# A six-layer fused kernel: the recurrence's k plus u is dropped, and the hand order of five engines is replaced

## The reference

```
x = x + attention_0(ln(x))        # 16 heads, weights rounded to -1, 0, 1
x = x + wkv(ln(x), ctx)           # a recurrence over the 128 tokens, per channel
x = x + ffn_0(ln(x))              # 704 hidden, weights rounded to -1, 0, 1
x = x + attention_1(ln(x))        # 32 query heads, 8 key heads
x = x + cross_attention(ln(x), ctx)
x = x + mixture(ln(x))            # low-rank experts, top 2 of 6
```

```
no = max(o, u + k);  A = exp(o - no);  E = exp(u + k - no)
y  = (A p + E v) / (A q + E)
no2 = max(w + o, k); A2 = exp(w + o - no2); E2 = exp(k - no2)
p, q, o = A2 p + E2 v, A2 q + E2, no2
```

## Time and profile before

| | |
|---|---|
| time, median of 3 runs | 685.28 us (684.7 to 687.41) |
| span of the profiled execution | 691.1 us |
| TensorE busy | 613.2 us (89%) |
| VectorE busy | 543.6 us (79%) |
| ScalarE busy | 481.4 us (70%) |
| GpSimd busy | 392.3 us (57%) |
| mean granted TensorE clock | 0.949 |

### The profile page before, as it was taken

One profiled execution on the slowest core, in us unless ns is written; L12 is line 12 of the kernel. 1 busy time (PEld: TensorE's weight loads), 2 busy tenths in 40 slices (PEclk: granted clock), 3 DMA queues, 4 the chain that ended last, 5 costly groups with the idle time before them and its releaser, 6 DMA issues.

```text
span 691.1 us, 20216 instructions
## 1 busy us (share of the span) xinstructions
PE 613.2 (89%) x7368; PEld 372.6 (54%) x7368; DVE 543.6 (79%) x1357; ACT 481.4 (70%) x1185; POOL 392.3 (57%) x745
## 2 busy tenths in 40 slices
PE   6699999856788789999999988789999999999984
PEld 6466666534566568544444344345555556555542
DVE  5889999899899996889998867567777777777521
ACT  4599998996878646577787773467676667666650
POOL 5343786897899958856665312334545544545321
PEclk9799999998899989999999999899999999999995
DMA  8899645111110002444545524353343444433000
GB/s 296 205 220 170 93 94 107 57 58 39 39 39 32 24 11 54 64 78 89 79 79 86 95 58 81 60 89 68 76 82 73 68 80 88 79 76 59 20 9 15
DMA packets 163603, 55.11 MB, mean 80 GB/s; under 512 B 148976, under 2 KB 161456, under 8 KB 163376
## 3 DMA queue, kind: packets, MB, share of 16 engines
q1 hardware_dynamic: 161456, 53.68, 38.1%
q0 software_dynamic: 2048, 0.14, 0.2%
HBM read 16.82 MB, written 5.24 MB: 32 GB/s over the span
## 4 chain that ended last, share of the span: by engine, by line
PE 57%; DVE 18%; issue 7%; POOL 6%; DMA 6%; ACT 4%; SPq 1%; DVEq 0%; ACTq 0%; POOLq 0%
PE bank L1333 4%; PE bank L1266 4%; PE bank L1002 3%; PE bank L1280 3%; PE bank L1678 3%; DMA l1x_qT<-l1x_neg_maxT 3%; DVE mix_num_den L1542 2%; PE bank L1355 2%; PE bank L1305 2%; DMA l1a_kT<-k_stack 2%; PE bank L1287 2%; PE bank L1863 2%; PE bank L976 2%; PE bank L1689 2%; PE bank L1022 2%
## 5 line engine op out<-in xcount | busy, mean ns | idle before, releaser
L1181 DVE TENSOR_REDUCE l1x_neg_max<-bank 128x2 f16<-128x448 f32 (+1 forms) x192 | 116.0, 640 | 46.3 <-PE bank L1287 46.1
L1235 ACT ACTIVATE l1x_probs<-bank 128x512 f32<-128x512 f32 x192 | 104.2, 596 | 57.4 <-PE bank L1309 33.0
L889 DVE TENSOR_REDUCE l1a_neg_max<-bank 128x4 f16<-128x512 f32 x128 | 82.2, 685 | 12.9 <-PE bank L976 11.9
L936 ACT ACTIVATE l1a_probs<-bank 128x512 f32<-128x512 f32 x128 | 69.5, 595 | 21.3 <-PE bank L990 21.3
L1137 POOL DMA_DIRECT2D l1x_qT<-l1x_neg_maxT x64 | 37.5, 592 | 51.7 <-ACT l1x_neg_maxT L1231 51.7
L1678 PE MATMUL bank<-mix_xT_parts,w_ternary 128*128 128x256 f16 x384 | 53.1, 287 | 7.7 <-DVE mix_hidden L1560 7.5
L1678 PEld LDWEIGHTS bank<-mix_xT_parts,w_ternary 128*128 128x128 f16 x384 | 38.5, 103 | 19.8 <-DVE mix_hidden L1560 11.2
L1754 POOL TENSOR_TENSOR moe_logits<-moe_low_rank_logits,router_bias 128x6 f32<-128x6 f32 x16 | 3.3, 206 | 77.4 <-ACT moe_low_rank_logits L1831 77.4
L573 DVE TENSOR_REDUCE l_neg_max<-bank 128x4 f16<-128x512 f32 x64 | 41.5, 674 | 5.7 <-PE bank L698 5.0
L1492 POOL TENSOR_TENSOR mix_hidden_parts<-mix_hidden,mix_hidden_parts 128x256 f16<-128x256 f32 x48 | 38.0, 799 | 8.5 <-ACT mix_hidden_parts L1623 8.1
L642 ACT ACTIVATE l_probs<-bank 128x512 f32<-128x512 f32 x64 | 35.2, 608 | 3.5 <-PE bank L721 1.8
(11 more groups left out here) (271 smaller groups left out, 1814.5 us busy)
## 6 DMA issues: line engine op xcount, KB each, us to landing
ctx_projected<-mix_ctx_projected SPq DMA_DIRECT2D x16, 192.0 KB, 2.0
l1x_ctx_projected<-ctx_projected SPq DMA_DIRECT2D x16, 160.0 KB, 2.4
mix_ctx_in<-ctx_in SPq DMA_DIRECT2D x16, 128.0 KB, 2.1
out_dram<-moe_out SPq DMA_DIRECT2D x16, 128.0 KB, 2.1
x_residual<-x_in SPq DMA_DIRECT2D x1, 1536.0 KB, 10.0
w_f<-w_in SPq DMA_DIRECT2D x2, 704.0 KB, 10.3
w_attn_f<-w_l_in SPq DMA_DIRECT2D x4, 256.0 KB, 3.9
q_stack<-q_begin_in SPq DMA_DIRECT2D x1, 1024.0 KB, 6.2
```

The lines of the kernel that those rows point to most:

```text
L889: dve.tensor_reduce(mm[:, 16 * j + 4 * s:16 * j + 4 * s + 4], b_s[c % 3][:].rearrange("p (r k) -> p r k", k=P), AX.X, ALU.max, negate=True ...
L936: act.activation(prob[:, c, :], b_st[c % 2][:], ACT.Exp).then_inc(s_exp, 1)
L1181: dve.tensor_reduce(mm[:, first:first + count], scores, AX.X, ALU.max, negate=True).then_inc(s_max, 1)
L1235: act.activation(prob[:, c, :], b_st[c % 2][:], ACT.Exp).then_inc(s_exp, 1)
```

## The change

It has three parts.

- k + u is no longer written. `W5` on GpSimd subtracts the running maximum from k itself. u moves into the guard: a tile `limit_minus_u` (60 - u, one column for each channel half, made once by GpSimd) is the bias of the Relu, which therefore runs once for each half.
- Three `F1c` pieces on GpSimd (the layer norm's power) get a further wait, for the normalised x of the sequence before last.
- `PHASES`, `PACE` and `STEPS` have new numbers for `mix`, `l1a`, `l1x` and `moe`, on all engines. `l0` keeps its own.

```
-    ku = sb("k_plus_u", [P, 2, 2, P])
+    spare = sb("limit_minus_u", [P, 2])
...
+        pool.tensor_tensor(spare[:], net.limit[:].to_broadcast([P, 2]), u, ALU.subtract).then_inc(s_c, 1)
...
-                pool.tensor_tensor(dif[:, c, 2], ku[:, c], prev, ALU.subtract).then_inc(s_da, 1)
+                pool.tensor_tensor(dif[:, c, 2], kx[:, c, :, 1:P + 1], prev, ALU.subtract).then_inc(s_da, 1)
...
-                for h in range(2):
-                    act.activation(ku[:, c, h, :], b_kv[c][:, P * h:P * h + P], ACT.Identity, bias=u[:, h:h + 1])
                 act.copy(kx[:, c, :, 1:P + 1], b_kv[c][:, 0:C].rearrange("p (h t) -> p h t", h=2))
...
-                act.activation(room[:, c], flat(dif[:, c, 2]), ACT.Relu, bias=net.limit[:],
-                               scale=-1.0).then_inc(s_ex, 1)
+                for h in range(2):
+                    ins = act.activation(room[:, c, P * h:P * h + P], dif[:, c, 2, h, :], ACT.Relu, bias=spare[:, h:h + 1],
+                                         scale=-1.0)
+                ins.then_inc(s_ex, 1)
...
+                wait(pool, s_xn, b - 1)
                 pool.tensor_tensor(rstd[:, bp, :], ve[:, bp, :], net.mhalf[:], ALU.pow).then_inc(s_rstd, 1)
...
     ("l1a", "pe"): phases("""
-        F5@-0.748 F7@-0.099 S.0@2.190 S.1@2.305 S.2@2.479 S.3@2.759 M@2.913 ST.0@3.547 ST.1@3.789 ST.2@4.136
```

More of the change, by code:

```diff
@@ L160 @@
     ("moe", "pe"): phases("""
[L161 removed]
+        TR@5.208 DOWN@5.245 LORA@5.711 UP@5.969"""),
 }
 PACE = {
[L164 to L168 removed]
+    "l0": (-91.729, 19.870, (4.716, 6.971, 8.492, 11.987), 11.788),
@@ L169 @@
+    "mix": (52.943, 9.367, (10.387, 13.342, 18.920, 10.211), 9.329),
+    "l1a": (155.583, 5.427, (8.962, 8.684, 11.231, 13.171), 11.184),
+    "l1x": (339.807, 9.660, (17.098, 4.845, 5.910, 27.874), 26.177),
+    "moe": (340.648, 2.496, (16.874, 4.857, 5.918, 27.835), 25.791),
 }
```

113 lines of the change are left out of this document (55 added, 58 removed).

## The result

The changed kernel takes 688.72 us in the median of 20 runs (686.58 to 692.53), the kernel before 686.58 us in 20 runs (683.48 to 689.94). The ratio is 1.0031, with a 95% interval of 1.0016 to 1.0046: 2.1 us slower, where I had forecast 3.6 us faster. The difference is smaller than the 0.5% that I called the bound of no change, but it is a difference, and of the other sign. The time lies in the range that I gave; its direction was wrong.

What follows compares the result with a forecast made beforehand. The limit was taken to change between ScalarE, VectorE, GpSimd and TensorE, with TensorE full from about 480 us. Terms -1.2 + 0.1 + 0 - 1.0 - 0.5 - 1.0 = -3.6 took 685.3 to 681.7 us; range 675.5 to 690.5.

Steps and rivals of the forecast that it cites:

- no change: Rival: VectorE and GpSimd take back the 1.2 us saved at the start of `mix`; 684.8 us, chance 0.25.
- Dropped k + u and the Relu halves: Start of `mix`: five Identities leave the chain (-1.61 us), two Relus in halves add 0.44; -1.2 us.
- GpSimd's subtraction: In `mix`, subtracting from k in rows of 129 takes 0.03 us longer, three such steps on the chain; +0.1 us.
- The new order in mix: In `mix`, new neighbours on VectorE and GpSimd neither better nor worse; 0 us, bounds -3.3 and +3.3.
- l1a: -1.0: In `l1a`, a later normalised x waits less for GpSimd's `F8b`; 0.1 us gained in each of ten turns.
- the filled wait: In `l1a`, statistics fill VectorE's wait for TensorE's last `S` before the last two reductions; -0.25 us a turn.
- Change to l1x: At the change to `l1x`, normalised x and statistics of the first sequences are drawn forward on VectorE; -0.5 us.
- l1x: -1.0: In steady `l1x`, the copy of the maxima goes earlier, shortening 12 waits of 8.9 us in all; -1.0 us.
- The slower one: Rival: in `l1a`, reciprocals wait for TensorE's transposes and hold up the work queued behind; 689 us, chance 0.18.
- The larger gain by shared ports: Rival: in `l1a`, normalised x starts ahead of or well behind `F8b`, taking 0.4 to 0.5 us; 676.9 us, chance 0.17.

Runs made afterwards that it cites:

- the four pairs: Four pairs of kernels differing by the change's code edits alone; the changed code was slower by 0.0012, 0.0022, 0.0023 and 0.0053 in ratio.
- the pause: The changed kernel with one wait added on GpSimd ahead of the fourth `W5`; ratio 1.0009 to the kernel before.
- before_again: The kernel before, unchanged, profiled a second time; span 683.8 us, where the first profile had 691.1.
- code_only: The kernel before with the change's code edits (no k + u, Relu halves, further `F1c` waits) but the old order tables; ratio 1.0012.
- padded_waits: The kernel before with the new order from the drain of `l1a` on, the further waits and 16 short copies in ScalarE's idle start; ratio 0.9994.

## Why the prediction was wrong

*Dropped k + u and the Relu halves: -1.2.* The chain passed through the Identities, but what followed them was not waiting for them alone: at equal clock they are worth 0.04 us at yT. I blamed the `l0` pieces of the new order in advance, but the saving is missing in the old order too. There the last D does come 1.5 us earlier without k + u (180.8 against 182.3 us), most of it by TensorE's clock in the head of `mix`; that this is about my size is luck. Over the whole kernel the four pairs have the changed code 0.0012 to 0.0053 slower. A Relu half was sized right (391 ns, where I had 368).

*GpSimd's subtraction: +0.1.* Its length was right (a median of 731 ns). I asked only how long one takes, and not where VectorE's sum comes to start beside it.

*The new order in mix: 0, measured +4.1 us with the changed code.* This is the step that failed. "I have no reason why the new neighbours should be better or worse", and a bound made from the median lengthening of all sixteen sums, could not see one sum of 4.72 us. And I added code and order as terms of their own, where the stall needs both. From the l0 row to D8 it is 182.3 us before (six profiles), 180.8 with the changed code (five), 182.8 with the new order (one), 184.9 with both (seven) and 183.2 with both and the pause (one). So of the 4.1 us between the same code in the two orders, the stalled sum is 1.7, read from one profile with the pause, and 2.4 are open in the main. 0.9 us come back at once, since `l1a`'s seventh normalised x starts 0.3 us ahead of D8 instead of 0.6 behind it. Against the kernel before the mix is 2.6 us longer, where my terms for it added up to 1.1 us less.

*l1a: -1.0, measured +1.7 us in nine turns.* I counted TensorE's `ST` pair ahead of `S` as 0.2 us and let the filled wait pay for it. It is most of the loss: 0.15 us in an undisturbed turn. The first turn adds 0.3 us, and one turn more waits for late keys (8.6 us in two turns, one before). The normalised x meets `F8b` as before (1340 ns), where I had counted on 0.9 to 1.2 us.

*Change to l1x: -0.5, measured -0.7* against `before_again` and -1.9 against the first profile of before, whose clock was lower there; at equal clock 0.3 to 0.8 us less, about my size.

*l1x: -1.0, measured -2.7 us in twelve turns.* The waits for the maxima did fall, but over the whole of `l1x` from 5.6 us in the second profile of before to 2.9; and `code_only`, in the old order, has 3.3 us in 9 cases and still 176.7 us for the twelve turns. The larger part, 1.7 us, is TensorE's busy time for the same number of instructions, for which I had no term: I had written that an order can only remove TensorE's waits there. So the sign was right and the mechanism only in part. In the tail it is +0.6 us against the second profile of before and -2.0 against the first, whose clock was lower there (0.85 against 0.94).

*The sum.* +2.6 - 0.9 + 1.7 - 0.7 - 2.7 + 0.6 = +0.6 us against the second profile of before, and +2.6 - 0.9 + 1.7 - 1.9 - 2.8 - 2.0 = -3.3 against the first, where the timing says +2.1 (1.1 to 3.2). The profiles therefore don't close the sum: the clock alone sets their stages some microseconds apart. Ahead of the l0 row nothing is lost that can be told from scatter (117.2 us in the mean of nine profiles with the new order, 116.8 in eleven with the old, between 115.5 and 119.1). The rest stays open. It is of the size of what `padded_waits` did, and so may be no more than where the instruction loads and the clock's steps fall; that is argued, not shown. By the ratios the same path reads: code +0.0012, new order in l1x -0.0017, in the drain -0.0018, in mix and l1a +0.0054, together +0.0031, each step uncertain by 0.003 to 0.004. So the loss in `mix` and `l1a` is what the ratios show best; how it divides between the two, they don't.

*The rivals.* None came true as told. The slower one had the right sign and the wrong place; that its 689 us was met is luck. The larger gain by shared ports looked at the normalised x, and what held VectorE up beside GpSimd was a sum in `mix`, with the opposite sign. The Trainium skill's page "SBUF — State Buffer", section "SBUF: two separate sides", says that the waiting engine "fully blocks" while the other holds the ports; taken for one instruction at a time, it would have held the sum to 138.6 us, the end of the GpSimd instruction that was running, or to 139.3 if the next came first. The trace shows the sum held on to the end of the last instruction of the train, 142.57; in `code_only` it was held for one instruction.

## What to carry to other kernels

Look for the longest instruction of a group, not only for its median: a VectorE instruction on SBUF that starts inside a train of GpSimd instructions without a gap may be held to the train's end, and one wait on GpSimd gave 3.3 us back at that point. Two edits that are harmless alone can put it there together, so test them together and apart. Judge an order stage by stage, and join the halves: here the first half of the new order lost and the second won, and joined they make a kernel 0.5 to 0.8% faster than before. And before explaining a microsecond, read the TensorE clock of that stretch in both profiles: 1.4 us that looked like saved work were four matmuls at the lower clock.

## What the runs showed of the hardware

- VectorE's 128x512 sum, 0.65 to 1.25 us otherwise, took 4.72 us in a gapless train of eight GpSimd instructions, and 4.69 and 4.63 us when it started 0.03 and 0.09 us later; it ended 0.55 us after the train each time, and 0.55 us after the last instruction ahead of an added pause (1.41 us). In trains as gapless in `code_only` and `order_only` the sum got its turn between two GpSimd instructions (1.25 and 0.69 us); what decides is open.
- In the old order of `mix`, 16 instructions fewer on ScalarE moved an instruction load by enough to delay a transposing transfer in another stage, at about 390 us, from 4.9 to 5.1 us to 5.6 to 5.7 us; 16 short copies put both back (5.1 us).
- The same stretch, with the same code and order up to there, ran at 1.2 or 2.4 GHz in different profiles, with TensorE's waits ahead of it alike (2.13 and 2.12 us); four matmuls of 128x384 took 2.77 or 1.46 us. In the drain the clock fell behind a wait of 0.61 us and stayed up behind one of 0.62. 16 copies of 0.1 us in ScalarE's idle start went with 0.0055 in the ratio in one pair of kernels and with nothing in the other. A difference of 0.3% between two builds is therefore weak evidence on any single edit.
